# Adding each block's expert rows into a table in DRAM by indirect scatters, and copying the table to the output

## The reference

```
u      = layernorm(x)
logits = u @ Wr.T                      # 8 experts
i, j   = the two experts with the largest logits, w = softmax of the two
y_e    = gelu(u @ Wi[e].T + bi[e]) @ Wo[e].T + bo[e]      # 192 -> 768 -> 192
out    = x + w[0] * y_i + w[1] * y_j
```

## Time and profile before

| | |
|---|---|
| median of 3 runs | 1255.05 us (1253.74 to 1255.72) |
| profiled execution: its time, its span | 1259.88 us, 1257.9 us |
| TensorE busy, share of the span | 825.4 us, 66% |
| VectorE | 921.5 us, 73% |
| ScalarE | 598.2 us, 48% |
| GpSimd | 362.2 us, 29% |
| last layer, from its first DMA issue | 1078.1 us to the end |
| its 15 blocks, first transpose of rows to last matmul | 1122.5 to 1227.0 us |

### The profile page before, as it was taken

One profiled execution on the slowest core, in us unless ns is written; L12 is line 12 of the kernel. 1 busy time (PEld: TensorE's weight loads), 2 busy tenths in 40 slices (PEclk: granted clock), 3 DMA queues, 4 the chain that ended last, 5 costly groups with the idle time before them and its releaser, 6 DMA issues. The chain is left out here.

```text
span 1257.9 us, 16849 instructions
## 1 busy us (share of the span) xinstructions
PE 825.4 (66%) x5554; PEld 576.7 (46%) x5554; DVE 921.5 (73%) x1731; ACT 598.2 (48%) x938; POOL 362.2 (29%) x309
## 2 busy tenths in 40 slices
PE   6799999859894041122224336599999747449990
PEld 2333333335783020011114225599888725339990
DVE  5679999936655989999993777488888533628871
ACT  3743333215331046789897223277766122328870
POOL 0036666430000822222210002532222510054444
PEclk8789999969997565555555676899999959659995
DMA  8075565130003000000000008299995110628932
GB/s 258 13 205 151 150 151 150 34 75 1 1 1 88 0 1 1 0 1 0 0 0 1 0 1 224 77 232 267 263 266 160 39 44 1 170 83 258 272 115 81
DMA packets 65821, 120.59 MB, mean 96 GB/s; under 512 B 11152, under 2 KB 40784, under 8 KB 65744
## 3 DMA queue, kind: packets, MB, share of 16 engines
q1 hardware_dynamic: 62672, 113.31, 33.4%
q0 software_dynamic: 3072, 6.30, 1.7%
HBM read 102.08 MB, written 17.50 MB: 95 GB/s over the span
## 5 line engine op out<-in xcount | busy, mean ns | idle before, releaser
L435 POOL TENSOR_TENSOR hC<-hs,Cb 128x1024 f32<-128x1024 f32 x47 | 110.7, 2355 | 129.3 <-DVE hs L472 129.3
L1726 POOL CAST m_h_hi<-m_h 128x512 f16<-128x512 f32 x62 | 54.0, 871 | 247.4 <-DVE m_h L1801 247.4
L472 DVE TENSOR_TENSOR_SCAN hs<-ps_l,dBu 128x1024 f32<-128x1024 f32 x48 | 110.0, 2291 | 2.8 <-ACT ps_l L550 1.2
L1440 PE MATMUL ps_l<-identb,q_pi 128*128 128x128 bf16 x192 | 29.2, 307 | 112.3 <-DVE q_pi L1243 112.3
L550 ACT ACTIVATE ps_l<-d_sp,Am 128x1020 f32<-128x1020 f32 x48 | 53.5, 1115 | 89.9 <-DVE hs L472 89.7
L615 PE MATMUL ps_l<-hC,selT 128*96 128x512 f32 x192 | 93.3, 609 | 1.5 <-POOL hC L435 1.5
L600 PE MATMUL ps_l<-du,sel 96*128 96x512 f32 x192 | 90.5, 593 | 1.4 <-DVE dBu L465 1.4
L1809 DVE TENSOR_TENSOR m_h_lo<-m_h,m_h_hi 128x512 f16<-128x512 f32 x62 | 42.8, 691 | 46.5 <-POOL m_h_hi L1726 41.9
L1121 POOL TENSOR_SCALAR q_e<-q_qi 128x512 int16<-128x512 bf16 x48 | 31.3, 652 | 153.7 <-DVE q_qi L1224 153.7
L1440 PEld LDWEIGHTS ps_l<-identb,q_pi 128*128 128x128 bf16 x192 | 16.5, 130 | 128.4 <-DVE q_pi L1243 128.4
L2092 PE MATMUL ps_m<-m_wd_hi,m_h_hi 128*128 128x192 f16 x248 | 62.9, 254 | 8.4 <-DVE m_h_lo L1809 4.8
(11 more groups left out here) (484 smaller groups left out, 2807.2 us busy)
## 6 DMA issues: line engine op xcount, KB each, us to landing
d_sp<-scan_d SPq DMA_DIRECT2D x48, 512.0 KB, 4.5
m_sta<-in_m_ua SPq DMA_DIRECT2D x25, 512.0 KB, 4.9
m_stb<-in_m_ub SPq DMA_DIRECT2D x50, 256.0 KB, 6.3
m_std<-in_m_dn SPq DMA_DIRECT2D x25, 384.0 KB, 8.2
g_std<-in_g_dn SPq DMA_DIRECT2D x15, 576.0 KB, 5.9
g_sta<-in_g_ua SPq DMA_DIRECT2D x15, 384.0 KB, 3.5
g_stb<-in_g_ub SPq DMA_DIRECT2D x30, 192.0 KB, 4.7
scratch_x<-zero SPq DMA_DIRECT2D x1, 4416.0 KB, 20.0
```

The costliest lines, as they stand in the source:

```text
L435: pool.tensor_tensor(hC[:, n % 2, :], hs[:, n % 2, :], Cb[:, which(n), :], ALU.mult).then_inc(weighted, 1)
L472: v.tensor_tensor_scan(hs[:, n % 2, ::step], dA(n)[:, ::step], dBu[:, n % 2, ::step], 0.0, ALU.mult, ALU.add).then_inc(scanned, 1)
L1726: pool.tensor_copy(h_hi[:, b % 2, q, :], src).then_inc(h_high, 1)
```

## The change

The last layer no longer stores and gathers its results. A DRAM table `sums` (256 + 1024 rows of 192 floats) gets the residual rows of X with the bias part, once. The row that travels through `scratch_x` becomes 8 numbers of 16 bits longer (XW = 392): they hold the token's row number in the table and the weight of this choice, so there is a second copy of U16 (`U16b`) for the second choice. `take` multiplies each row by its weight, now in two instructions. `add_rows(n)` on GpSimd issues two indirect scatters of 128 rows with addition into `sums` for each block, two blocks behind, inside the loop of casts; those of the last two blocks follow after the loop. Empty slots carry zeros and are sent to the 256 spare rows. Each `add_rows` waits until the one before has landed. SyncE at last copies the table to the output in four DMAs. `xg` gets 5 buffers, and is loaded anew only when the block's rows have been added. Both expert layers get 5 more semaphores, the last one 2 more for xg; the first layer fills its 8 new columns with zeros.

```diff
-XW = 3 * P
+XT = 3 * P
+XW = XT + 8
...
@@ load_rows (SyncE)
-                    if n >= 3:
-                        sync.wait_ge(turned, n - 2)
+                    if n >= NX:
+                        if gated:
+                            sync.wait_ge(turned, n - NX + 1)
+                        else:
+                            sync.wait_ge(summed, 32 * (n - NX + 1))
...
+                    sync.dma_start(tok[:, :], D["tok"][:, :]).then_inc(loaded, 16)
...
-                    if 0 <= b - 2 < STEPS and plan[b - 2].kind == "routed":
+                    if b == -1 and not gated:
+                        for n in range(2):
+                            sync.dma_start(K["sums"][n * P:(n + 1) * P, :], K["zero"][:, 0:2 * C].bitcast(F32)).then_inc(base, 16)
+                        sync.wait_ge(bias_added, NT // 2)
+                        sync.dma_start(K["sums"][BS:BS + T, :].rearrange("(t p) c -> p t c", p=P), X[:, :, :]).then_inc(base, 16)
+                    if gated and 0 <= b - 2 < STEPS and plan[b - 2].kind == "routed":
                         store(plan[b - 2].arg)
                 if out is not None:
-                    for t in range(NT):
-                        sync.wait_ge(combined, min(2 * t + 3, 2 * NT))
-                        sync.dma_start(out[t * P:(t + 1) * P, :], X[:, t, :]).then_inc(out_done, 16)
+                    sync.wait_ge(summed, 32 * ROUTED)
+                    for n in range(4):
+                        rows = slice(n * T // 4, (n + 1) * T // 4)
+                        sync.dma_start(out[rows, :].rearrange("(p a) c -> p (a c)", p=P),
+                                       K["sums"][BS + n * T // 4:BS + (n + 1) * T // 4, :].rearrange("(p a) c -> p (a c)", p=P)
+                                       ).then_inc(out_done, 16)
...
@@ GpSimd
+                        if gated:
+                            pool.memset(U16[:, :, XT:XW], 0.0).then_inc(tail, 1)
+                        else:
+                            pool.tensor_copy(U16b[:, :, 0:XT], U16[:, :, 0:XT]).then_inc(copied, 1)
...
+                def add_rows(n):
+                    pool.wait_ge(taken, 2 * n + 2)
+                    pool.wait_ge(rowed, n + 1)
+                    if n == 0:
+                        pool.wait_ge(base, 48)
+                    else:
+                        pool.wait_ge(summed, 32 * n)
+                    for i in range(2):
+                        pool.indirect_dma_start(out=K["sums"][:, :],
+                                                out_offset=bass.IndirectOffsetOnAxis(ap=to_row[:, n, i:i + 1], axis=0),
+                                                in_=o_sb[:, n % 2, i, :], in_offset=None, compute_op=ALU.add).then_inc(summed, 16)
...
                     high(k)
+                    if not gated and k % PAIRS == 0 and k >= 2 * PAIRS:
+                        add_rows(k // PAIRS - 2)
+                if not gated:
+                    add_rows(ROUTED - 2)
+                    add_rows(ROUTED - 1)
-                while back < 2 * NT:
+                while gated and back < 2 * NT:
                     gather(back // 2, back % 2)
...
@@ VectorE, after wts and before the slots
+                    for j, rows in enumerate((U16, U16b)):
+                        step(v.tensor_copy(rows[:, :, XT:XT + 2].bitcast(F32), tok[:, 2:2 + NT].unsqueeze(2)))
+                        step(v.tensor_scalar(rows[:, :, XT + 2:XT + 4].bitcast(F32), wts[:, :, j:j + 1], 1 / WS, None, ALU.mult))
+                        step(v.memset(rows[:, :, XT + 4:XW], 0.0))
...
@@ VectorE, each block (and no more weighted sums into X at the end)
+                    if not gated:
+                        v.wait_ge(x_in[b % NX], 16 * (b // NX + 1))
+                        v.tensor_tensor(to_row[:, b, :].unsqueeze(2), xg[b % NX][:, :, XT:XT + 2].bitcast(F32), tok[:, 0:2].unsqueeze(2), ALU.max).then_inc(rowed, 1)
...
@@ take (ScalarE)
+                    if not gated:
+                        if n >= 2:
+                            act.wait_ge(summed, 32 * (n - 1))
+                        for i in range(2):
+                            act.activation(o_sb[:, n % 2, i, :], ps[:, 6 + b % 2, i * BS:i * BS + C], ACT.Copy,
+                                           scale=xg[n % NX][:, i, XT + 2:XT + 4].bitcast(F32)).then_inc(taken, 1)
+                        return
```

More of the change, by code:

```diff
@@ L356, in idle @@
                     for _ in range(count):
-                        pe.matmul(ps[:, 5, 0:XW], const["zero"][:, 0:P], const["zero"][:, :], start=True, stop=True)
+                        pe.matmul(ps[:, 5, 0:XT], const["zero"][:, 0:P], const["zero"][:, 0:XT], start=True, stop=True)
                 pe.wait_ge(zeroed, 1)
@@ L1581, in expert_layer @@
         U16 = ctx.sb(f"{pre}_U16", [P, NT, XW], F16)
+        U16b = U16 if gated else ctx.sb(f"{pre}_U16b", [P, NT, XW], F16)
+        tok = None if gated else ctx.sb(f"{pre}_tok", [P, 2 + NT])
+        to_row = None if gated else ctx.sb(f"{pre}_to_row", [P, ROUTED, 2], I32)
         xd = ctx.sb(f"{pre}_xd", [P, 4, PARTS_X, BS], F16)
@@ L1618, in expert_layer @@
         bias = ctx.sb(f"{pre}_bias", [P, 4, tiles])
-        xg = [ctx.sb(f"{pre}_xg{a}", [P, 2, XW], F16) for a in range(3)]
+        NX = 3 if gated else 5
+        xg = [ctx.sb(f"{pre}_xg{a}", [P, 2, XW], F16) for a in range(NX)]
         xt = [ctx.sb(f"{pre}_xt{a}", [P, PARTS_X, BS], F16) for a in range(2)]
@@ L1625, in expert_layer @@
         o_sb = ctx.sb(f"{pre}_o", [P, 2, 2, C])
-        got = ctx.sb(f"{pre}_got", [P, NT, 2, C])
+        got = ctx.sb(f"{pre}_got", [P, NT, 2, C]) if gated else None
         bo = ctx.sb(f"{pre}_bo", [routed, C])
@@ L1634, in expert_layer @@
         b_in = [S(f"b_in{a}") for a in range(4)]
-        x_in = [S(f"x_in{a}") for a in range(3)]
+        x_in = [S(f"x_in{a}") for a in range(NX)]
         stored = [S(f"stored{a}") for a in range(2)]
@@ L1646, in expert_layer @@
         combined, out_done = S("combined"), S("out_done")
+        base, summed, tail, copied = S("base"), S("summed"), S("tail"), S("copied")
+        rowed = S("rowed")
+        LOADS = 64 if gated else 96
         WD = 4
@@ L1842, in _ @@
                 step(v.tensor_copy(bestf[:], besti[:]))
-                v.wait_ge(loaded, 64 if gated else 80)
+                v.wait_ge(loaded, LOADS)
                 grid = iota[:, :].unsqueeze(1).broadcast_to([P, NT, routed])
@@ L1916, in _ @@
                     v.wait_ge(added, shared_before(STEPS))
-                if not gated:
-                    v.wait_ge(bias_added, NT // 2)
-                for t in range(NT):
+                for t in range(NT if gated else 0):
                     v.wait_ge(gathered[t], 32)
@@ L1925, in _ @@
                                                ).then_inc(combined, 1)
[L1926 to L1929, removed]
+                if gated:
+                    v.wait_ge(combined, 2 * NT - 1)
+                    v.scalar_tensor_tensor(X[:, NT - 1, :], got[:, NT - 1, 1, :], wts[:, NT - 1, 1:2], X[:, NT - 1, :], ALU.mult, ALU.add
+                                           ).then_inc(combined, 1)
+                    v.wait_ge(combined, 2 * NT)
             @block.scalar
@@ L1950, in _ @@
                 ln.scalar(act, use)
-                act.wait_ge(loaded, 64 if gated else 80)
+                act.wait_ge(loaded, LOADS)
                 act.activation(ga[:, 0, :], ga_f[:, :], ACT.Copy, scale=WS).then_inc(gate_hi, 1)
@@ L2039, in turn @@
                     n = plan[b].arg
-                    pe.wait_ge(x_in[n % 3], 16 * (n // 3 + 1))
+                    pe.wait_ge(x_in[n % NX], 16 * (n // NX + 1))
                     if n >= 2:
@@ L2084, in down_block @@
                         if plan[b - 2].kind == "routed":
-                            pe.wait_ge(taken, plan[b - 2].arg + 1)
+                            pe.wait_ge(taken, (plan[b - 2].arg + 1) * (1 if gated else 2))
                         else:
@@ L2315, in program @@
              "before": ctx.sb("before", [P, P], BF16), "all": ctx.sb("all", [P, P], BF16),
-             "scratch_x": nc.dram_tensor("scratch_x", (SLOTS, XW), F16, kind="Internal").ap(),
+             "scratch_x": nc.dram_tensor("scratch_x", (SLOTS, XW // 2), I32, kind="Internal").ap(),
+             "sums": nc.dram_tensor("sums", (BS + T, C), F32, kind="Internal").ap(),
              "scratch_y": nc.dram_tensor("scratch_y", (SLOTS, C), F32, kind="Internal").ap(),
@@ L2437, in _layouts @@
     o["before"] = f(p[:, None] < p[None, :])
+    o["tok"] = f(p[:, None] + P * np.arange(2 + NT)[None, :])
     o["first"] = con(np.tile(BS * np.arange(16, dtype=np.float32), (P, 1)))
```

14 lines of the change are left out of this document (8 added, 6 removed).

## The result

The changed kernel takes 1278.21 us, the median of 4 runs (1274.70 to 1285.28), beside 1254.67 for the kernel before on the same chip. The ratio is 1.0194, with a 95% interval of 1.0150 to 1.0239: it is slower, by about 24 us (1.9%), where 14 us less were forecast.

What follows compares the result with a forecast made beforehand. It saw 30.8 us behind the last matmul, about 20 of them gather issue, as what to shorten. Sum: -15.5 + 1.1 + 0.3 = -14.1 us, off the 1255.05 median: 1241.0 us, range 1236 to 1254.

Steps and rivals of the forecast that it cites:

- (b): Last layer's blocks: each pair of scatters waits for the previous landing, up to 4.87 us before GpSimd stalls; costed at nothing.
- A: Time from the start of an indirect scatter with addition until it has landed: bounded by 2.4 and 5.0 us, 3.3 taken.
- threshold: In the blocks, the landing time above which GpSimd stalls: 4.87 us, period 6.58 less 1.71 between scatter starts.
- The term for the instruction: GpSimd in the blocks: scatters with addition issue as fast as plain ones, 0.95 us; a pair takes 2.84, hidden.
- the later casts: Last block: the pair of block 12 stands before the second cast; last matmul +1.0 us, at 1228.1.
- Serial landings: Rival, chance 0.14: in the blocks, waiting for the previous pair's landing sets the period; at 7 us landing, +19, 1274.
- Issuing costs more: Rival, chance 0.10: addition takes 1.9 us on GpSimd, +13 in 12 blocks, +3 at end, about 1257; 1.3 is hidden.
- Some stall: Rival, chance 0.22: accumulation is slow beside weights; landing 5.5 us in 8 blocks, +6, 1247; 1243 to 1252 overall.
- the forecast: Likeliest case, chance 0.50: the end shrinks and the blocks hide the additions, -14.1 us; alone 1237 to 1245.
- The end: Behind the last matmul: two pairs and four table copies replace the gathers; span ends at 1242.4, 15.5 us less.
- the four copies: At the end, SyncE's table-to-output copies: issued 0.47 us apart, landed between 1237.5 and 1239.1, 1238.2 taken.
- VectorE's steps: Last layer's front: six new small steps before the slot numbers delay the scatters and everything after, +1.1 us.

Runs made afterwards that it cites:

- two tables: Changed kernel with even and odd blocks adding into separate tables, xg freed early, second table left out of output: 1253.63 us, ratio 0.9972 to the kernel before.
- rows of their own: Changed kernel with plain scatters to a separate row per token and choice, both choices loaded and added at the end: 1250.78 us, ratio 0.9953 to the kernel before.
- variant with two queues: Plain scatters to separate rows, with loads of choice 1 and half the output stores moved to ScalarE's queue: 1253.83 us, ratio 0.9973 to the kernel before.

## Why the prediction was wrong

**The step that failed** is (b) of what hides in the blocks, and behind it the bounds of A. The mechanism was seen: a pair waits for the landing before, GpSimd stalls when A is over a threshold, and its casts, the low halves and TensorE follow. Its size was not. A was bounded by 2.4 and 5.0, and both came from rows of idle queues (that an addition takes no longer than a scatter and a gather one after the other was an estimate of mine; no run shows such rounds), though a row of the same prediction had the way out: stores of 192 KB took 5.2 us beside weights and 1.97 alone. I set that factor aside because those stores stood behind weights in their own queue. The runs show that a separate queue doesn't protect: 3.8 to 4.1 us with no weights, 5.0 to 5.6 with 768 KB, 6.7 to 7.7 with 1344. Applying the store's factor of 2.6 to the value I took, 3.3, is an estimate of 8.7, well over the threshold.

**The threshold was too generous as well.** 4.87 was 6.58 - 1.71. The wake of 0.69 us after each landing was missing, and the two starts lie 1.88 to 2.4 apart, not 1.71. The room was 6.58 - 1.9 - 0.7 = 4.0. Even A without any weights, 3.4 to 4.1, left 0.6 of it at best, and nothing at worst.

**The term for the instruction** (0.95) was mis-sized: 1.56 at the end, 1.6 to 2.7 in the blocks. The pairs on GpSimd cost 9 of the 36.7 us: 7.3 in the steady blocks, by their length, since plain ones leave 0.9 there, and 1.7 in the last block, where plain ones cost 1.8 by standing before the casts. 27 are the wait beside the weights (141.3 - 114.2), and weights alone add none (114.2 - 114.7). The last us is the first block's slow clock and no part of the change. In the last block the sum had the later casts at +1.0, an estimate that no run shows; they were +1.7 (5.75 us from `take` to `take` for 4.03). "Both scatter and gather took 0.95, which speaks for equal times" did not carry over to the addition.

**The rivals.** *Serial landings*, at 0.14, had the mechanism: the pair's landing sets the period. It gave 1274 for A = 7, and 1278 was measured, but that its number is so near is in part luck. It put 7.4 us into the end for A = 7 there, where A was 3.5 and the end cost 3.3, and it left out the longer instructions, 9 us. Its 25.6 us for the blocks stand beside 27. *Issuing costs more*, at 0.10, was true too: its two cases were 1.3 and 1.9 us, the blocks had 1.6 to 2.7, and it cost 9 us where it set 13 for 1.9. *Some stall* had the right place, but with A = 5.5 it priced 6 us. It, the forecast and *serial landings* are one mechanism at three values of A, and the chances among them were given by rows of idle queues.

**The end** was forecast at 14.3 us behind the last matmul and took 17.6. About 1.3 of the 3.3 us are the pair of block 13. It had to wait for the landing of the pair before and started 3.1 us before the last `take`, not 4.0; its second instruction came 1.88 after the first instead of 1.7, and landed after 3.5 instead of 3.3. Another 1.3 are the last pair: 0.75 instead of 0.2 from landing to start, 1.87 instead of 1.25 from start to start, and 0.2 of A. The rest are the four copies, +0.9, less small gains at SyncE's wake and the clearing. SyncE's queue in time and its waits have them:

```profile
1274.40 2.48 SPq L1729 DMA_DIRECT2D out<-sums  x4
...
SPq L1659 <- DMA out<-sums: 2.5, 1, 2.5
```

They were issued 0.63 apart for 0.47, and had landed at 1279.4 (the last issue ended at 1276.88, and SyncE then waited 2.5), 5.0 us after the first was issued, for 4.1. No run shows by itself the 2.0 us of latency in the forecast's upper value for these copies: a store of 192 KB took 1.97 in all. The clearing, 1283.5 - 1279.4 = 4.1, is as forecast (4.2).

**Right:** +1.1 us of VectorE's steps, the copy on GpSimd and the longer rows hidden, A on idle queues (3.3 for 3.4 to 3.5), no gathers. The test that I set, "wrong if the period is over 6.6, if an instruction of `add_rows` lasts over 1.3 us, or if A is over 4.9", failed in all three parts.

**The clock** does not set the period. The mean granted clock fell from 1.00 to 0.93: in some blocks, after TensorE had stood idle, a slice of 4 us shows 0.57 to 0.80 (0.61 from 1200 to 1204, for one, with 0.50 in each microsecond from 1200 to 1203). The landing that the next pair waited for came at 1203.47 (1195.99 + 7.48), and that pair started at 1204.23, as long after the landing as the other pairs, so it waited for the landing and not for TensorE. Outside the steady blocks the clock does count: 0.8 us of the 36.7 lie before the first `take`, where TensorE, after 14 us of waiting for rows, ran at 0.50 for 5 us of its first block's matmuls and not for 3.

## What to carry to other kernels

Before a DMA is made a link in a chain that runs once a block, price its landing beside the traffic of that stage, not from a row at the end of the kernel: here the same instruction landed after 3.4 us alone and up to 7.7 us beside 1344 KB of weights, although it had a queue of its own. Accumulation into one table, with each pair waiting for the landing of the pair before, cost 27 us here (blocks of 141.3 us, and 114.2 with two tables); if rows can be given places of their own, writing them and adding once at the end keeps a gain without the chain (ratio 0.9953 here). When no engine is full and the DMA engines swing between full and empty (shares of 1.09 and 0.00 in the same period here), look for one wait that all stand behind, and move it with a second buffer before anything is made faster.

No run here adds into one table without the wait, so it is not shown whether it could just be dropped; the version with rows of their own has no addition and so no such wait, while two tables halve the chain and need a second addition at the end.

## What the runs showed of the hardware

- An indirect scatter with addition of 128 rows of 768 bytes keeps GpSimd busy for 1.56 us, the plain one for 0.96; in the blocks, beside the other engines, 1.6 to 2.7 and 1.0 to 2.1.
- It lands 3.4 to 3.5 us after its start on idle queues, the plain one 2.3 to 3.1. Beside 1344 KB of loads a block in another queue it is 6.7 to 7.7 and 3.2 to 4.8.
- It makes 144 packets where the plain one makes 48 for the same bytes (6624 for 3744 with 30 of them), and 0.54 us more of the mean DMA engine.
- GpSimd goes on 0.69 us after such a landing.
- The releaser that the profile names for a wait on several semaphores was wrong for 5 of these pairs; the start on another queue that waits for the same semaphore alone (L1694) showed the true one.
- TensorE's granted clock can fall within one block, and idle time alone does not say whether it does: before the last `down_block` TensorE stood idle for 2.7 us both with rows of their own and in its variant with two queues; the first began at 0.50 and took 4.65 us, the second stayed at 1.00 and took 3.17.
